# A two-layer recurrent network on one core per sequence: layer 0's FFN computed by features, and layer 1's normalisation with it

## The chip, the cores and the metric

The kernel runs on 8 cores of one Trainium2 chip. Each core takes one of the eight sequences (4096 tokens of 1024 features) through both layers, and the cores do not talk to each other. The metric is the device time of the slowest core in microseconds (us). The engines are named as the profile names them: PE is TensorE, PEld its weight loads, DVE is VectorE, ACT is ScalarE, POOL is GpSimd, SP is SyncE.

## The reference, cut to what matters

```python
# x: (8, 4096, 1024) float32; every kernel input is float32, layer 1's FFN weights int32
xn = _layernorm(x)                          # no scale, no bias
# layer 0: gates from block-diagonal linears, then a closed-form scan over time
gate_x = sigmoid(block_diag_linear(xn, w_in, b_in)); gate_a = sigmoid(block_diag_linear(xn, w_a, b_a))
a = minimum(exp(-gate_a * (softplus(a_param) + 0.001)), 1 - 1e-5)
s = closed_form_rnn_scan(xn * gate_x * sqrt(maximum(1 - a*a, 1e-5)), a)
g = silu(gelu(xn @ ternary(W1).T + b1) @ ternary(W2).T + b2)      # 1024 -> 4096 -> 1024
x = x + s * g
# layer 1
xn = _layernorm(x)
u  = _layer_norm(xn, gamma, beta)           # a second normalisation, over the first
zxbcdt = u @ W_in + b_in                    # z 2048 | x 2048 | B 64 | C 64 | dt 8 columns
s = xn + mamba2(...)                        # scan with 8 heads, silu(z), @ W_out + b_out
g = silu((silu(xn @ wg) * (xn @ wu)) @ wd)  # 1024 -> 3072 -> 1024, weights / 127
x = x + s * g
```

`ternary(W)` rounds to -1, 0 or 1 with a threshold from the mean of |W| over the whole matrix, so no matmul with W1 can begin before all of W1 has been read.

## The kernel before, in words

Everything is written out by hand in one function. There is no scheduler: each engine has a queue, and an instruction stands in it where the Python code appended it. Tokens (a semaphore and a count) say what an instruction waits for; `P.dma(queue, slot, out, in, *tokens)` puts a transfer on SP's or POOL's queue, and whatever stands behind it on that queue waits with it. Matrices are bf16 in SBUF; in 32 slots of 4 KB per partition lie first W1 as float32 (`raw`), then ternary W1 in the lower halves (`Lh`) and ternary W2 in the upper ones (`Hh`). The 4096 tokens go in 8 blocks of 512, a block in 4 tiles of 128.

**Start.** SP loads 4 tiles of x and the 32 tiles of W1; DVE and ACT sum absolute values (`w1_sum`, L281, L285). Between the sums block 0 is normalised, transposed by TensorE (L350) and its gates are computed (`a_gates`): for each of the 8 feature groups two gate matmuls, tanh into one of two buffers `thx`, and a store to `gt` in HBM by POOL. Block 0's gates stand between the sums, one after each third weight tile. A short chain on one partition splits b2 into three bf16 rows (L460 to L466). Then the threshold (L294), and W1 becomes ternary.

**Stage A**, per block: the up projection, L386: 32 feature tiles of 8 matmuls of 128 x 512, gelu by ACT into `hst`, stored to `h1` in HBM. The next block's normalisation and gates, and W2's sum and thresholding, run beside it. In the last block `b_early` runs block 0's recurrence and issues the first load of `h1`.

**Stage B**, the down projection by tokens: `b_down(n, hf)` for 32 tiles of 128 tokens and 2 halves of the features. The tile's `h1` is the stationary operand, W2 moves: 32 matmuls of 512 columns (L693) and one with three rows that adds b2 (L696). `b_tail` brings the recurrence's result, which lies by features, into token order with four fp32 transposes (L708), then silu on ACT (L715), product and residual on DVE (L716, L718), and stores x1 by tokens. Beside it DVE and ACT run the recurrence of the next block, one feature group per group of matmuls: `b_recA` (limited sum and difference, L555, L557), `b_recM` (L566 to L568) and `b_recC` (L576 to L580), with its gate inputs loaded by SP. POOL loads `Win` into the lower halves.

**Stage C**, 8 blocks: `c_ln` reads a tile of x1, takes its statistics (L760, L761), and derives both normalisations, 1/sqrt by pow on POOL (L768); `c_trans` transposes both results in bf16 by TensorE (L782), into `uT` for this stage and, by HBM, `xn1` for layer 1's FFN. For block 0 that happens in the last groups of stage B, for block b+1 in block b. A block's matmuls: dt and B/C columns (`c_small`, L882, L891), 16 groups for z (`c_z`, L915, evacuated by ACT to `zs`), 16 for x (`c_xs`, L932, evacuated by DVE to `xs`, L939), 8 matmuls of 512 columns each. In blocks 0 and 1 POOL also loads half of the gate and up weights (`gu_load`), cast from int32.

**Stages D and E**: the scan by chunks of 128 tokens with the matmuls of layer 1's FFN between them, then the two last projections and the sum. The change touches only the layout in which they read `xn1`.

The functions that the change touches:

## Time and profile before

| | |
|---|---|
| median of 3 runs | 2956.08 us (2955.19, 2956.08, 3278.76) |
| the profiled execution | 2955.45 us, its span on the slowest core 2953.6 us |
| spans of the eight cores | 2945.9 to 2953.6 us |
| granted TensorE clock, mean of a core | 0.987 to 0.995 of full |
| busy: PE, DVE, ACT, POOL | 2824.4, 1614.8, 1210.4, 334.3 us |
| moved by DMA | 515.04 MB, 174 GB/s over the span |
| start, to the threshold matmul | 0 to 87.96 us |
| stage A | to 606 us |
| stage B | 606.58 to 1110.70 us |
| stage C | 1110.70 to about 1630 us |
| gate loads and h1 loads, median to landing, whole run | 6.7 us, 6.4 us |
| casting weight loads issued from 1110 to 1200 us | 26 |
| waits on stores of xs before L939, whole run | 56.3 us in 35 |

The profile is one execution on the slowest core. An instruction's row names its line, engine, operation, and output<-inputs by the program's names. TensorE's matmuls are pipelined: a matmul of 512 columns is shown 0.38 us long, while eight of them start within 1.72 us, so what one costs is read from the starts. The brackets at a row's end tell how long the engine had been idle before it and what it waited for.

### The profile page before, as it was taken

How to read it: one execution, taken by the hardware profiler on the slowest of the kernel's cores; microseconds unless marked ns; L12 is line 12 of the kernel's file. 1: busy time of each engine (PE TensorE's matmuls, PEld its weight loads, DVE VectorE, ACT ScalarE, POOL GpSimd, SP SyncE). 2: the span in 40 equal slices, each digit the busy share in tenths (PEclk: the TensorE clock that was granted, in tenths of full speed). 3: DMA queues.
4: the chain of work that ended last, by engine and by line, in shares of the span. 5: the costliest groups of instructions: out<-in, count | busy, mean ns of one | idle time of the engine just before them, and what ended most of it. 6: DMA issues, size and time to landing. Idle time of an engine off the chain costs nothing.

```text
span 2953.6 us, 39109 instructions; the slowest of 8 cores (2945.9 to 2953.6 us)
## 1 busy us (share of the span) xinstructions
PE 2824.4 (96%) x14022; PEld 1330.5 (45%) x14222; DVE 1614.8 (55%) x2865; ACT 1210.4 (41%) x1806; POOL 334.3 (11%) x550
## 2 busy tenths in 40 slices
PE   2699999999999998999999999999999999999998
PEld 0244444444444444444444444444444444444443
DVE  4755576567777743444443666666666623333333
ACT  3665555777777733344432334333333300000000
POOL 1011121001110012100000122111111110000000
PEclk9999999999999999999999999999999999999999
DMA  9388887567897557533433666445564453433342
GB/s 285 112 251 269 270 266 240 165 210 222 229 242 227 191 185 166 147 108 119 127 113 111 194 172 182 154 141 171 164 182 139 150 161 136 144 137 128 143 146 76
DMA packets 269684, 515.04 MB, mean 174 GB/s; under 512 B 23476, under 2 KB 143028, under 8 KB 265272
## 3 DMA queue, kind: packets, MB, share of 16 engines
q1 hardware_dynamic: 208216, 338.16, 36.4%
q0 software_dynamic: 61280, 174.38, 20.5%
q8 instruction: 117, 1.92, 0.3%
q14 instruction: 71, 0.58, 0.1%
HBM read 359.89 MB, written 184.82 MB: 184 GB/s over the span
## 4 chain that ended last, share of the span: by engine, by line
PE 89%; DMA 4%; DVE 3%; ACT 2%; issue 1%; POOL 0%; SPq 0%; DVEq 0%; POOLq 0%; ACTq 0%
PE ps L693 14%; PE ps L386 14%; PE ps L1200 11%; PE ps L1206 11%; PE ps L1328 10%; PE ps L1341 7%; PE ps L932 7%; PE ps L915 6%; PE ps L708 1%; DMA zs<-zst 1%; PE ps L1082 1%; DMA gt<-thx 1%; PE ps L1088 1%; PE ps L782 1%; PE ps L350 1%
## 5 line engine op out<-in xcount | busy, mean ns | idle before, releaser
L386 PE MATMUL ps<-xnT,Lh 128*128 128x512 bf16 x2001 | 454.9, 382 | 9.6 <-ACT hst L390 3.8
L693 PE MATMUL ps<-Hh,h1s 128*128 128x512 bf16 x2000 | 449.3, 379 | 3.3 <-DMA h1s<-h 0.8
L1328 PE MATMUL ps<-Hh,hl 128*128 128x512 bf16 x1510 | 339.9, 379 | 1.4
L386 PEld LDWEIGHTS ps<-xnT,Lh 128*128 128x128 bf16 x2048 | 201.1, 98 | 241.7 <-issue 16.9
L693 PEld LDWEIGHTS ps<-Hh,h1s 128*128 128x128 bf16 x2048 | 200.1, 98 | 228.7 <-issue 1.5
L1203 ACT ACTIVATE sg<-ps 128x512 bf16<-128x512 f32 x192 | 111.3, 596 | 418.1 <-PE ps L1200 381.8
L1208 DVE TENSOR_TENSOR hgs<-sg,ps 128x512 bf16<-128x512 bf16 x192 | 131.5, 685 | 269.8 <-PE ps L1206 155.0
L1352 ACT ACTIVATE gx<-ps 128x512 f32<-128x512 f32 x64 | 38.2, 597 | 512.4 <-DVE sx L1354 501.6
L390 ACT ACTIVATE hst<-ps,cons 128x512 bf16<-128x512 f32 x256 | 172.7, 688 | 184.1 <-PE ps L386 161.6
L915 PE MATMUL ps<-uT,Lh 128*128 128x512 bf16 x1000 | 226.6, 381 | 7.9 <-ACT zst L918 5.4
L1328 PEld LDWEIGHTS ps<-Hh,hl 128*128 128x128 bf16 x1536 | 150.3, 98 | 181.2
L932 PE MATMUL ps<-Lh,uT 128*128 128x512 bf16 x1000 | 224.6, 380 | 4.7 <-DVE xst L939 3.1
L1351 DVE TENSOR_TENSOR sx<-sx,ps 128x512 f32<-128x512 f32 x64 | 44.1, 689 | 338.2 <-PE ps L1341 337.9
L1341 PE MATMUL ps<-Lh,yl 128*128 128x512 bf16 x756 | 185.5, 379 | 2.2 <-DMA Lh<-Wo 1.6
L1200 PE MATMUL ps<-xg,Hh 128*128 128x512 bf16 x768 | 181.8, 379 | 0.0
L1200 PE MATMUL ps<-xg,Lh 128*128 128x512 bf16 x768 | 181.7, 379 | 0.0
L1206 PE MATMUL ps<-xg,Hh 128*128 128x512 bf16 x768 | 181.4, 379 | 0.0
L1206 PE MATMUL ps<-xg,Lh 128*128 128x512 bf16 x768 | 181.4, 379 | 0.0
L939 DVE TENSOR_TENSOR xst<-ps,bx 128x512 bf16<-128x512 f32 x128 | 86.8, 690 | 133.9 <-PE ps L932 75.4
L915 PEld LDWEIGHTS ps<-uT,Lh 128*128 128x128 bf16 x1024 | 99.0, 98 | 124.4 <-issue 10.0
L932 PEld LDWEIGHTS ps<-Lh,uT 128*128 128x128 bf16 x1024 | 99.6, 98 | 122.4 <-issue 7.0
L101 POOL DMA_DIRECT2D hg<-hgs x96 | 73.0, 760 | 709.9 <-DVE hgs L1208 654.3
(209 smaller groups left out, 3683.7 us busy)
## 6 DMA issues: line engine op xcount, KB each, us to landing
gt<-thx POOLq DMA_DIRECT2D x64, 512.0 KB, 4.3
h<-hst SPq DMA_DIRECT2D x128, 256.0 KB, 3.9
wst<-W2T POOLq DMA_DIRECT2D x64, 512.0 KB, 5.7
h1s<-h SPq DMA_DIRECT2D x32, 1024.0 KB, 6.4
hg<-hgs POOLq DMA_DIRECT2D x96, 256.0 KB, 4.8
hl<-hg SPq DMA_DIRECT2D x32, 768.0 KB, 5.1
xt<-x SPq DMA_DIRECT2D x32, 512.0 KB, 7.0
raw<-W1T SPq DMA_DIRECT2D x32, 512.0 KB, 22.2
```

What stands on the lines that cost most here:

```text
L386: t = PE.do(lambda e, dc=dc: e.matmul(psum[i][:], Lh[(ft // 8) * 8 + dc][:, (ft % 8) * 128:(ft % 8 + 1) * 128], xnT[b % 2][:, dc, :], star ...
L390: pf[i] = ACT.do(lambda s: s.activation(hst[j][:, :, ft % 2, :], psum[i].rearrange("p (c t) -> p c t", t=128), AF.Gelu, bias=b1s[:, ft:ft ...
L693: PE.do(lambda e, f=f: e.matmul(psum[bk][:], H[:, f, :], Hh[f][:, hf * 512:(hf + 1) * 512], start=(f == 0), stop=False), h1_tok[n], pf[bk] ...
L915: t = PE.do(lambda e, dc=dc: e.matmul(psum[i][:], winp(dc, ft * 128, 128), U[:, dc, :], start=(dc == 0), stop=(dc == 7)), pf[i], tok=(dc = ...
L932: t = PE.do(lambda e, dc=dc: e.matmul(psum[i][:], U[:, dc, tt * 128:(tt + 1) * 128], winp(dc, 2048 + fb * 512, 512), start=(dc == 0), stop ...
L939: pf[i] = DVE.do(lambda v: v.tensor_add(xst[j][:], psum[i][:], bx[:, fb * 512:(fb + 1) * 512]), t, *xst_free[j], t_bx)
L1200: t = PE.do(lambda e, dc=dc: e.matmul(psum[i][:], gu(p, 0, dc, ft), X[:, :, dc, :], start=(dc == 0), stop=(dc == 7)), xg_tok[n], t_gu[p], ...
L1203: pf[i] = ts = ACT.do(lambda s: s.activation(sg[i][:], psum[i][:], AF.Silu, scale=1.0 / 127.0), t, sg_free[i], *endC)
L1206: t = PE.do(lambda e, dc=dc: e.matmul(psum[2 + i][:], gu(p, 1, dc, ft), X[:, :, dc, :], start=(dc == 0), stop=(dc == 7)), pf[2 + i], tok=( ...
L1208: pf[2 + i] = sg_free[i] = DVE.do(lambda v: v.tensor_mul(hgs[j][:, :, ft % 2, :], sg[i].rearrange("p (c t) -> p c t", t=128), psum[2 + i]. ...
L1328: td = PE.do(lambda e, f=f: e.matmul(psum[bd][:], hl[i][:, f, :], wd[f][:, sl], start=(f == 0), stop=(f == 23)), e_tok[(1, n)], t_wd, pf[b ...
L1341: to = PE.do(lambda e, f=f: e.matmul(psum[bo_][:], yl[i][:, f, :], wo[f][:, sl], start=(f == 0), stop=(f == 15)), e_tok[(0, n)], t_wo, pf[ ...
```

## The change

The down projection is turned round: W2's 128 x 128 tile is stationary and h1 moves, 256 tokens at a time, so that its result, like the recurrence's, lies by features. Two such groups of 32 matmuls share a PSUM bank. b2 becomes a bias of the silu, which now works inside PSUM; no bias matmul, no fp32 transposes of the recurrence. The residual x is read from a copy that the host has transposed (`xT`), and x1 is stored by features (`x1t`), in pieces of 1 KB. `h1` is kept in chunks of 256 tokens, stored in pieces of 1 KB rather than 512 bytes; two chunks of 2 MB lie in SBUF where W1 was.

The recurrence works in pairs of feature groups, with four gate buffers and four `rd` buffers from block 1 on and two `cl`; POOL copies the carries. The minimum in `b_recM` is gone.

Layer 1's normalisation works by features: `c_stat` reads a feature tile of x1, transposes it to tokens by TensorE in fp32, takes statistics of each 128 features, copies it out with ACT and stores it by tokens for the last stage; `c_rows` joins the statistics, transposes mean and both factors into rows, and brings them through HBM to all partitions; `c_app` reads the feature tile again and applies them on DVE. All of its loads and stores are on POOL's queue. In stage C the x groups come before the z groups, since the last z columns of `Win` are loaded only after stage B has freed h1's space. At the start there are four gate buffers for block 0, two of them in the space of x tiles 4 and 5, and the work on b2 is gone.

```diff
-    thx = [at(f"thx{i}", [128, 2, 512], F32, T0 + 4096 * i) for i in range(2)]
+    thx = [at(f"thx{i}", [128, 2, 512], F32, o)
+           for i, o in enumerate((T0, T0 + 4096, X0 + 16384, X0 + 20480))]
...
-        j = k % 2
+        j = k % 2 if b else k % 4
...
-    xfree[4] = xfree[5] = thx_free[0] = t_b2d
...
+    xfree[4], xfree[5] = thx_free[2:]
...
-            h1_tok[n] = P.dma(SP, s_h1[n % 2], h1s[n % 2][:], h1_d[n], h1_free[n % 2], *h1st[n // 4])
+            h1_tok[n] = P.dma(SP, s_h1[n % 2], h1s[n % 2], h1_d[n].rearrange("p (a f) t -> p a (f t)", a=8),
+                              h1_free[n % 2], *h1st[n // 2])
...
-    def b_down(n, hf):
-        g = n * 2 + hf
-        bk = g % 4
-        H = h1s[n % 2]
-        for f in range(32):
-            PE.do(lambda e, f=f: e.matmul(psum[bk][:], H[:, f, :], Hh[f][:, hf * 512:(hf + 1) * 512],
-                                          start=(f == 0), stop=False),
-                  h1_tok[n], pf[bk], t_w2[f], tok=False)
-        t = PE.do(lambda e: e.matmul(psum[bk][:], on3[:], b2s[:, hf * 512:(hf + 1) * 512], start=False, stop=True),
-                  t_on3, t_b2)
+    def b_down(g):
+
+        hb, p = divmod(g, 4)
+        bk = g % 6
+        H = h1s[hb % 2].rearrange("p a (f t) -> p a f t", t=256)
+        for e in range(2):
+            fb = 2 * p + e
+            for f in range(32):
+                t = PE.do(lambda q, f=f, fb=fb, e=e: q.matmul(
+                    psum[bk][:, e * 256:(e + 1) * 256], Hh[f][:, fb * 128:(fb + 1) * 128], H[:, f // 4, f % 4, :],
+                    start=(f == 0), stop=(f == 31)),
+                    h1_tok[hb], pf[bk], t_w2[f], tok=(f == 31 and e == 1))
...
+    def c_stat(b, k):
...
+        for c in range(4):
+            t = PE.do(lambda e, c=c: e.transpose(psum[bk][:, c * 128:(c + 1) * 128],
+                                                 xq[i][:, c * 128:(c + 1) * 128], idf[:]),
+                      xq_tok[j], pf[bk], tok=(c == 3))
+        for c in range(4):
+            td = DVE.do(lambda v, c=c: v.bn_stats(sst[:, c, k, :], psum[bk][:, c * 128:(c + 1) * 128]), t, st_prev[0])
+        sst_tok[b] = td
+        t = pf[bk] = ACT.do(lambda s: s.activation(xq[i][:], psum[bk][:], AF.Copy), td)
...
+    def c_app(b, k):
...
+        t = DVE.do(lambda v: v.tensor_sub(X[:], X[:], rows[:, 0, :]), xq_tok[j], row_tok[b])
+        tx = DVE.do(lambda v: v.tensor_mul(xb[k % 2][:], X[:], rows[:, 1, :]), t, *xb_free[k % 2])
+        tu = DVE.do(lambda v: v.tensor_mul(U, X[:], rows[:, 2, :]), *uT_free[b % 2])
...
+            if last == 3:
+                for k in range(4 * e, 4 * e + 4):
+                    c_app(0, k)
+                    if e == 0:
+                        c_load()
...
+    while win_todo:
+        b_winload(PE.last())
...
+    for _ in range(5):
+        c_load()
...
         for q in range(32):
...
+            if b + 1 < NB:
+                if q in (0, 1, 2, 3, 4, 9, 10, 11):
+                    c_stat(b + 1, (0, 1, 2, 3, 4, 9, 10, 11).index(q))
+                if q in (5, 6, 7, 8, 9, 13, 14, 15):
+                    c_load()
+                if q == 12:
+                    c_rows(b + 1)
+                if q in (20, 21, 23, 24, 26, 27, 29, 30):
+                    c_app(b + 1, (20, 21, 23, 24, 26, 27, 29, 30).index(q))
+                    c_load()
```

How the orders change, at three places. On TensorE in stage B, between two groups, before (`sv` holds the recurrence, `Hh` is W2):

```order
L693 MATMUL ps<-Hh_137,h1s_195 128x512
L693 MATMUL ps<-Hh_138,h1s_195 128x512
L696 MATMUL ps<-b2s,on_202 128x512
L708 MATMUL ps<-idf,sv_188 128x128 [waits s_act]
L708 MATMUL ps<-idf,sv_188 128x128 x3
L693 MATMUL ps<-Hh_107,h1s_195 128x512
L693 MATMUL ps<-Hh_108,h1s_195 128x512
```

and in the changed kernel, where `WW` holds h1:

```order
L708 MATMUL ps<-WW,Hh_139 128x256
L708 MATMUL ps<-WW,Hh_140 128x256
L708 MATMUL ps<-WW,Hh_109 128x256 [waits s_act]
L708 MATMUL ps<-WW,Hh_110 128x256
L708 MATMUL ps<-WW,Hh_111 128x256
```

Nothing stands between two groups any more, and each group is 32 matmuls of 256 columns. On POOL where stage B ends, before (from the last stores of x1 to the first weights of layer 1's FFN):

```order
L101 DMA x<-xr_198 128x512 [waits s_dve]
L101 DMA x<-xr_196 128x512 [waits s_dve]
L768 TENSOR_TENSOR ssm<-ssm,mhalf 128x2 [waits s_dve]
L101 DMA Hh_107<-wgT 128x1024 [waits s_pe]
L101 DMA Hh_108<-wgT 128x512
```

and changed (`xn<-xb` stores a normalised tile, `Lh<-Win` loads columns of z, `xq<-x1t` feature tiles of x1 for block 1's statistics):

```order
L101 DMA xn<-xb_219 128x512 [waits s_dve]
L101 DMA xn<-xb_220 128x512 [waits s_dve]
L101 DMA Lh_81<-Win 128x1024
L101 DMA Lh_82<-Win 128x1024
L101 DMA Lh_83<-Win 128x1024
L101 DMA Lh_84<-Win 128x1024
L101 DMA x1t<-xr_197 128x2x256 [waits s_dve]
L101 DMA x1t<-xr_195 128x2x256 [waits s_dve]
L101 DMA Lh_89<-Win 128x1024 [waits s_pe]
L101 DMA Lh_90<-Win 128x1024
L101 DMA Lh_91<-Win 128x1024
L101 DMA Lh_92<-Win 128x1024
L101 DMA xq_214<-x1t 128x512 [waits d_xo2,d_xo0]
```

Before, layer 1's loads had the queue to themselves from here on; now eight loads of `Win` and the tiles of x1 stand in it, behind stores that wait for DVE. On DVE in block 0 of stage C, changed, around `c_rows` (L814 to L829; L1032 evacuates an x group, L805 takes statistics):

```order
L805 BN_STATS sst<-ps 128x6 [waits s_pe]
L805 BN_STATS sst<-ps 128x6 x3
L1032 TENSOR_TENSOR xst_225<-ps,WWf 128x512 [waits s_pe,d_xs1]
L814 BN_AGGR smv<-sst 128x2 [waits s_dve]
L814 BN_AGGR smv<-sst 128x2 x3
L817 COPY st_237<-smv 128x4 [waits s_dve]
L818 COPY mu_all<-smv 128x4
L821 TENSOR_SCALAR ssm<-smv 128x4
L822 TENSOR_SCALAR ssm<-smv 128x4
L826 COPY r_all<-st_237 128x4 [waits s_pool]
L829 COPY srow<-ps 12x128 [waits s_pe]
L1032 TENSOR_TENSOR xst_224<-ps,WWf 128x512 [waits s_pe,d_xs0]
```

and on TensorE at the same place:

```order
L1027 MATMUL ps<-Lh_99,uT_221 128x512
L1027 MATMUL ps<-Lh_100,uT_221 128x512
L827 MATMUL ps<-idf,st_237 12x128 [waits s_pool,s_dve,s_act]
L1027 MATMUL ps<-wn_205,uT_221 128x512
L1027 MATMUL ps<-wn_206,uT_221 128x512
```

The statistics of a whole block are joined behind the evacuation of the group that TensorE has just finished, and TensorE's next group stands behind their transposition.

## Rows read from the trace of the kernel before

**Rows 1.** The page: busy time of each engine; chain that ended last, by engine

```profile
PE 2824.4 (96%) x14022; PEld 1330.5 (45%) x14222; DVE 1614.8 (55%) x2865; ACT 1210.4 (41%) x1806; POOL 334.3 (11%) x550
...
PE 89%; DMA 4%; DVE 3%; ACT 2%; issue 1%; POOL 0%; SPq 0%; DVEq 0%; POOLq 0%; ACTq 0%
```

**Rows 2.** Timeline of PE, down stage: start us, us, engine, line, operation, output<-inputs, count

```profile
809.80 7.07 PE L693 MATMUL ps<-Hh,h1s 128*128 128x512 bf16 x31
816.81 0.38 PE L696 MATMUL ps<-b2s,on 3*128 3x512 bf16 x1
817.12 0.66 PE L708 MATMUL ps<-idf,sv 128*128 128x128 f32 x4
817.61 7.07 PE L693 MATMUL ps<-Hh,h1s 128*128 128x512 bf16 x32
```

**Rows 3.** Timeline of all engines where the down stage begins

```profile
599.85 0.33 SPq L101 DMA_DIRECT2D h1s<-h  x1
...
606.58 7.07 PE L693 MATMUL ps<-Hh,h1s 128*128 128x512 bf16 x32 [0.78 <-DMA h1s<-h]
```

**Rows 4.** Timeline of PE where projection blocks begin

```profile
1110.70 1.67 PE L882 MATMUL ps<-uT,wtl 128*8 128x512 bf16 x7
...
1187.04 1.89 PE L882 MATMUL ps<-uT,wtl 128*8 128x512 bf16 x8
...
1565.97 1.89 PE L882 MATMUL ps<-uT,wtl 128*8 128x512 bf16 x8
```

**Rows 5.** DMA queues, window 1110 to 1200, and timeline of ACT there

```profile
q0 software_dynamic: 3616, 5.24, 37.4%
q1 hardware_dynamic: 8432, 8.69, 31.6%
...
1137.07 1.27 ACT L918 ACTIVATE zst<-ps,cons 128x512 bf16<-128x512 f32 x2 [6.87 <-DMA zs<-zst]
```

**Rows 6.** Timeline of the start; windows: engines' busy us (count), clock, DMA share, GB/s

```profile
69.72 1.27 ACT L367 ACTIVATE thx<-ps,cons 128x512 f32<-128x512 f32 x2 [8.49 <-DMA gt<-thx]
...
87.96 0.56 PE L294 MATMUL ps<-acc,onesf 128*128 128x1 f32 x2 [4.91 <-DVE acc L290]
...
78.00:82.00 4.00, 0.11 (x1) 0.10 (x1) 0.22 (x1) 0.94 (x2) 0.00 (x0) 1.00 0.98 395
```

**Rows 7.** Timeline of PE, 512, 256 and 128 columns; weight loads, ns min/median/max

```profile
1655.80 1.89 PE L1206 MATMUL ps<-xg,Hh 128*128 128x512 bf16 x8
1657.52 0.27 PE L1082 MATMUL ps<-Cx,stb 128*128 128x256 bf16 x1
1657.63 0.28 PE L1088 MATMUL ps<-sct,xsc 128*128 128x128 bf16 x2
...
1657.96 1.89 PE L1200 MATMUL ps<-xg,Hh 128*128 128x512 bf16 x8
...
L1082 PEld LDWEIGHTS ps<-Cx,stb x256: 95/98/98, 1630.0 to 2377.9; 128*128 128x128 bf16 x128
```

**Rows 8.** Timeline of DVE in the down stage; landing times of the gate loads

```profile
642.01 1.28 DVE L555 TENSOR_TENSOR_SCAN cl<-gv,car,par 128x512 f32<-128x512 f32 x1
643.33 0.69 DVE L557 TENSOR_TENSOR rd<-cl 128x512 f32<-128x512 f32 x1
...
644.01 0.69 DVE L576 TENSOR_TENSOR sv<-sv,gv 128x512 f32<-128x512 f32 x1
...
645.20 1.28 DVE L580 TENSOR_TENSOR_SCAN sv<-rd,sv,sv 128x512 f32<-128x512 f32 x1
...
DMA to landing us min/median/max: 4.4/6.9/9.8
```

**Rows 9.** Timeline where the down stage ends; one group of PE by line

```profile
1087.57 0.21 DVE L761 BATCH_NORM_AGGREGATE smv<-sst 128x2 f32<-128x12 f32 x1
...
1088.99 0.81 DVE L769 TENSOR_SCALAR ub<-xc,smv,ssm 128x1024 bf16<-128x1024 f32 x1 [0.90 <-POOL ssm L768]
...
L782 PE MATMUL ps<-idb,ub 128*128 128x128 bf16 x256 | 19.5, 219 | 0.0
```

506 lines of the change are left out of this document (280 added, 226 removed).

## The prediction, made before the changed kernel ran

> **What bounds the kernel now.** I read the page first: TensorE is busy 96% of the span, and 89% of the chain that ended last is matmuls [rows 1]. So only three things count: columns that TensorE streams, instructions that stretch them, and stretches in which it waits. I went through the stages with the timeline.
>
> The down stage is a stream: 32 matmuls of 512 columns take 7.01 us (809.80 to 816.81), then come a bias matmul and four fp32 transposes, and the next group starts 7.81 us after the last [rows 2]. 64 such groups and some layer norm fill 606.58 to 1110.70, 504.1 us [rows 3, 4]. The projection blocks behind it start at 1110.70, 1187.04 and, the eighth, 1565.97 [rows 4]: the first takes 76.3 us, the next six 378.9 us, 63.2 each. So the first loses 13 us. There ScalarE stood 6.87 us on a store of zs, while 26 casting weight loads held the q0 queue for 37.4% of 90 us [rows 5]: 1.3 us of all engines for each. At the very start TensorE does next to nothing until the threshold matmul at 87.96; ScalarE had waited 8.49 us for a gate buffer to be stored [rows 6].
>
> The durations are of the profiled execution (2955.45 us; the median of the runs is 2956.08, so the two are interchangeable).
>
> **1. The start.** Two gate buffers become four, and 4.5 us of VectorE work on b2 go. But behind the gates stand the loads of W1: the DMA engines are at 0.98 up to 82 [rows 6]. By 82 us they had moved the weights, six gate stores and two early x tiles. The x tiles queue behind the weights, the two gate stores now pulled ahead compete with them, so the last weight tile lands at 79 to 82. A sum, the total and the threshold follow in about 2 us: 82.5 for 88, **-5.5** (from -2 to -9). The x tiles 4 and 5 now wait for the gates' stores, near 85 us; they are used after 105, so this costs nothing.
>
> **2. Into the down stage.** The first h1 load was issued at 599.85, and TensorE started at 606.58 after a wait of 0.78 us [rows 3]. It is 2 MB now instead of 1: at the 3.3 us per MB of q1 (8.69 MB in 31.6% of 90 us) [rows 5], that is 3 us later. **+2.5** (0 to 5).
>
> **3. The down stage.** 2048 matmuls of 512 columns become 4096 of 256, each with its own weight load; 64 bias matmuls and 256 transposes go. The price of a 256-column matmul with full weights stands in the trace: two of them and four of 128 columns, 1024 columns in six instructions, take 0.44 us (1657.52 to 1657.96), against 1.72 us for eight of 512 [rows 7]. By columns that is 0.110 us for 256; half of a 512 is 0.1075. I take 0.1095, nearer to the first: 4096 x 0.1095 = 448.5 us. No row shows such a stream lasting more than six instructions, so the range keeps 0.1075 (440) to 0.115 (471).
> Added: 32 fp32 transposes for block 0's statistics at 0.49/4 us [rows 2]: 3.9. They come four tiles in a row on two PSUM banks, so the third waits for four statistics and a copy of the first, about 1.75 us, twice: 3.5 (0 to 6). The transposition in c_rows sits behind a group of 7 us and its inputs are ready: 0.
> Then the end. VectorE has the normalisation of eight tiles behind the tail of group 61: three fp32 operations each, 0.69 us [rows 8], so 8 x 2.07 = 16.6 us, from 2.4 us into the last pair of groups, and its bf16 stores stand on POOL's queue behind four weight loads, 2.5 us more. The pair takes 14 us, so the first projection waits 8.5 us with the copy (0 to 12). Sum: 448.5 + 3.9 + 3.5 + 8.5 = 464.4 against 504.1, **-39.7**.
> On VectorE a pair of steps costs 2 x 1.97 (scan, difference), 2 x 2.47 (product, addition, scan) and 2 x 1.4 (tail) = 11.6 us [rows 8], inside 14. Copies of carries go to POOL, which is 11% busy. Six PSUM banks give the tails two pairs of slack.
>
> **4. Projection block 0.** POOL's order is the point: the last eight Win tiles stand there behind the stores of the normalised tiles and the last tails, and the five x1 tiles that block 1's statistics need stand behind those. Eight tiles at 1.67 us (1.3 scaled from the mean of 202 KB to 256) are 13 us from about 7 us behind the stage's end; the x1 tiles land at about 24. TensorE has 12 us of its own before (8.5 waiting, 3.5 of c_small), so it waits **12 us** at the first transposition. After that each of the 16 x steps asks for a weight load (1.3), an x1 store or load (0.9) and an xs store (0.4): 2.6 to 2.7 us of DMA against 1.73 of TensorE, 43 us; the z steps ask for 2.0, 32 us; c_rows 3. Block: 3.5 + 12 + 43 + 3 + 32 = 93.5 against 76.3, **+17.2** (from -10, if all of it is hidden, to +54).
>
> **5. Blocks 1 to 6.** Transposes: 64 of bf16 (0.076 us busy each, 19.5 us for 256) against 32 of fp32 at 0.12 [rows 2, 9]: nothing. But c_rows puts one transposition between two groups of TensorE that needs a chain begun after the group before it: its evacuation on VectorE (0.8 with the wait), four aggregates, two copies, two small operations, and pow on POOL. The same chain for one tile took 1.42 us, 1087.57 to 1088.99 [rows 9]; three more aggregates are 0.6. So 2.8 us in each, x 6 = **+16.8** (0 to 25). The other work fits: VectorE has 1.5 us in a step of 2.2 that carries statistics.
>
> Moved without effect: in front of D and later, layouts alone change. Sum: -5.5 + 2.5 - 39.7 + 17.2 + 16.8 = -8.7, so 2955.45 - 8.7 = **2946.7 us**. What the FFN gives, the new layer norm takes back.
>
> **Rivals.**
> *A, all hidden.* Start -9, down stage 448.5 + 3.9 (-51.7), block 0 at 66 us (-10), rows free: -71, **2884 us**. For it: TensorE is the only full engine. Against it: the orders above.
> *B, VectorE's loop through the gate loads bounds the down stage; the side of slower.* A gate buffer is freed by the product of pair m and refilled for the scan of pair m+2, the first thing VectorE does next. The loop is 8.1 us of VectorE's work and the load: from a load of 5.9 us on it exceeds 14. The loads took 4.4, 6.9 and 9.8 us (minimum, median, maximum) there [rows 8], beside 1 MB loads ahead of them on the same queue. At 6.9 a pair takes 15.0: 30 x 1.0 = +30, **2977 us**; at 9.8, +117, 3064. Against it: the h1 loads go out before every second pair only, and with nothing ahead the minimum applies.
> *C, DMA binds the projections.* Stores of xs have two buffers of one step each. If each of the eight pairs of x steps is held 6.87 us longer, as ScalarE once was by a store [rows 5], they take 28 + 55 = 83 us, 40 more than in the sum, and block 1 half of that: 2947 + 60 = **3007 us**. For it: half the buffer of zs, in the time of the densest loads. Against it: POOL issues the weight loads behind its x1 work, so they thin out when the steps slow down.
> *D, weight loads don't hide.* A weight load of such a matmul lasts 98 ns [rows 7]. Shown bare, it adds 4096 x 0.098 = 401 us: **3348 us**. The row of six instructions in 0.44 us speaks against it: six loads alone would be 0.59. The Trainium skill says, in "TensorE: Matmul & The Clock Gate", under The mechanism, that a weight load overlaps matmuls in flight only when its row group differs; all here use all rows, and by that rule this change would be a disaster. The trace disagrees already in its 512-column stream. The same page gives, under Back-to-back issue gap, sustained pairs of about 81 ns for 128 columns and 131 ns for 512; an estimate from that page for 256 is 98 ns between them, which would make the sum 47 us less. The trace disagrees with that too: its 512 columns take 0.215 us.
> That the diff does not do what it says: the orders show the matmuls, so 2%, with no time.
>
> **Chances.** Main case 48%, A 17%, B 18%, C 13%, D 2%, other 2%. The main case's own range is 2925 to 2970. The range for 8 in 10 leaves out the ends of A and B and C's worse half: **2890 to 2990**. 2% of the time is 59 us, what a measurement here separates surely: faster than 2897 takes nearly all of A, 15%; slower than 3015 takes B's long loads, part of C, and D: 8%; within, 77%.
>
> **What would show it.** Step 1: the threshold matmul at 82 to 83. Step 3: 64 matmuls of the new down line in 7.0 us, no idle time between groups; if VectorE's scans there wait for gv for over 2.4 us a pair, B is on. A wait of 8 us before the first projection, on VectorE or ScalarE (uT). Step 4: 12 us of TensorE at the first transposition of xq, waiting for its load, and idle TensorE on xst in block 0. Step 5: some 3 us of idle TensorE in front of the transposition of the statistics, seven times, and projection blocks of 66 us. The prediction is wrong if the blocks stay at 63, or if 256 columns take more than 0.115 us.

## The result, and the profile of the changed kernel

The changed kernel takes 3022.77 and 3013.82 us, beside 2955.19 to 2957.74 before: a ratio of 1.021, with a 95% interval of 1.0172 to 1.0247. It is slower, by some 62 us; whether by more than 2% the runs leave open. (Some executions of either kernel, in which the cores of a die show a lower clock, take up to 3346.66 us; the times below are all of the others.) The prediction was 2947, with a range of 2890 to 2990. The profiled execution is the one of 3022.77 us, span 3020.9, so it stands 67.3 us above the profiled one of before.

First the page: totals, the granted clock in 40 slices, the chain that ended last by engine, and two groups of instructions.

```profile
PE 2802.6 (93%) x15474; PEld 1509.7 (50%) x15702; DVE 1632.2 (54%) x2875; ACT 1136.7 (38%) x1686; POOL 571.3 (19%) x987
...
PEclk7799999999999988999999999999999999999999
...
PE 70%; DMA 14%; DVE 9%; ACT 2%; SPq 2%; issue 2%; POOL 1%; DVEq 0%; POOLq 0%; ACTq 0%
...
L708 PE MATMUL ps<-WW,Hh 128*128 128x256 bf16 x4096 | 451.8, 274 | 5.3 <-DMA WW<-h 5.3
...
L556 DVE TENSOR_TENSOR_SCAN cl<-gv,cl,par 128x512 f32<-128x512 f32 x64 | 81.9, 1279 | 100.9 <-DMA gv<-gt 99.2
```

TensorE is busy 22 us less than before [rows 1] in a span 67 us longer, and matmuls hold 70% of the chain that ended last, for 89% before. The clock row has two 8s where block 0 of the projections lies, and two 7s at the start; the same row of before has 9s in all 40 places. Then the boundaries, from TensorE's timeline (start us, us, line, tiles, count, idle before and its releaser):

```profile
607.63 4.56 PE L708 MATMUL ps<-WW,Hh 128*128 128x256 bf16 x21 [4.76 <-DMA WW<-h]
...
889.61 56.05 PE L708 MATMUL ps<-WW,Hh 128*128 128x256 bf16 x512 [0.24 <-DMA WW<-h]
...
1023.83 2.18 PE L801 MATMUL ps<-idf,xq 128*128 128x128 f32 x8 [7.85 <-DMA xq<-x1t]
...
1056.69 0.27 PE L827 MATMUL ps<-idf,st 128*12 128x128 f32 x1 [1.83 <-DVE r_all L826]
...
1092.31 3.57 PE L976 MATMUL ps<-uT,wtl 128*8 128x512 bf16 x8 [14.39 <-ACT ps L721]
...
1109.50 1.09 PE L801 MATMUL ps<-idf,xq 128*128 128x128 f32 x4 [11.38 <-DMA xq<-x1t]
...
1199.98 3.57 PE L976 MATMUL ps<-Lh,wtl 128*8 128x512 bf16 x8 [3.21 <-ACT Lh L846]
...
1633.60 1.89 PE L976 MATMUL ps<-Lh,wtl 128*8 128x512 bf16 x8
```

They answer to [rows 3, 4]. The ledger for the slowest core, core 6 in both, with the prediction's terms:

| part | predicted | measured | from |
|---|---|---|---|
| start, to the threshold matmul | -5.5 | -3.7 | 87.96 to 84.26 |
| from there to the down stage | +2.5 | +4.7 | the stage starts at 607.63 for 606.58 |
| down stage, to block 0 | -39.7 | -19.4 | 484.7 us for 504.1 |
| projection block 0 | +17.2 | +31.3 | 107.7 for 76.3 |
| blocks 1 to 6 | +16.8 | +54.7 | 433.6 for 378.9 |
| the rest | 0 | -0.3 | 1387.3 for 1387.6 |
| sum | -8.7 | +67.3 | |

Cores differ more than they did. In the kernel before, all reach their eighth block between 1555.9 and 1566.0; in the changed one between 1603 and 1634. Already where the down stage ends the changed kernel's cores lie from 1070.4 to 1092.6, for 1106.4 to 1111.1 before; the slowest core's stage is 19.4 us shorter, the median one's 27.1 (476.6 for 503.7). So the median core is used beside the slowest from here on; for it block 0 takes 104.7 us (before 72.6), block 1 76.8 (63.3), and blocks 2 to 6 70.7 each (63.0).

### The profile page after: what moved, and what is told of

Read it like the earlier page. It is cut to its first block, busy times and chain, and to the rows that moved or that the text cites. A ratio compares the mean times of both kernels' runs of the same rounds, so it can differ in the third digit from the quotient of the medians.

```text
span 3020.9 us, 42623 instructions; the slowest of 8 cores (2994.9 to 3020.9 us)
## 1 busy us (share of the span) xinstructions
PE 2802.6 (93%) x15474; PEld 1509.7 (50%) x15702; DVE 1632.2 (54%) x2875; ACT 1136.7 (38%) x1686; POOL 571.3 (19%) x987
## 4 chain that ended last, share of the span: by engine, by line
PE 70%; DMA 14%; DVE 9%; ACT 2%; SPq 2%; issue 2%; POOL 1%; DVEq 0%; POOLq 0%; ACTq 0%
PE ps L387 13%; PE ps L1297 11%; PE ps L1303 11%; PE ps L1426 11%; PE ps L1439 7%; PE ps L1008 6%; PE ps L1027 5%; DMA gv<-gt 5%; DMA xs<-xst 3%; SPq L101 2%; DVE cl L556 1%; DMA xr<-xT 1%; DVE xr L733 1%; PE ps L1175 1%; DMA xq<-x1t 1%
## 5 line engine op out<-in xcount | busy, mean ns | idle before, releaser
L708 PE MATMUL ps<-WW,Hh 128*128 128x256 bf16 x4096 | 451.8, 274 | 5.3 <-DMA WW<-h 5.3
L708 PEld LDWEIGHTS ps<-WW,Hh 128*128 128x128 bf16 x4096 | 402.3, 98 | 54.6 <-issue 6.2
L1032 DVE TENSOR_TENSOR xst<-ps,WWf 128x512 bf16<-128x512 f32 x128 | 87.7, 690 | 185.1 <-DMA xs<-xst 94.6
L1012 ACT ACTIVATE zst<-ps,cons 128x512 bf16<-128x512 f32 x128 | 87.0, 685 | 185.7 <-PE ps L1008 148.3
L556 DVE TENSOR_TENSOR_SCAN cl<-gv,cl,par 128x512 f32<-128x512 f32 x64 | 81.9, 1279 | 100.9 <-DMA gv<-gt 99.2
L1303 PEld LDWEIGHTS ps<-xg,Hh 128*128 128x128 bf16 x768 | 75.2, 98 | 90.6
L1439 PEld LDWEIGHTS ps<-Lh,yl 128*128 128x128 bf16 x768 | 75.1, 98 | 90.6
```

Of the source, the lines that this page charges most:

```text
L556: tc = DVE.do(lambda v: v.tensor_tensor_scan(L[:, 2:514], G[:], lim, L[:, 1:2], op0=ALU.add, op1=ALU.min), gv_tok[n], ci_tok[n])
L708: t = PE.do(lambda q, f=f, fb=fb, e=e: q.matmul(psum[bk][:, e * 256:(e + 1) * 256], Hh[f][:, fb * 128:(fb + 1) * 128], H[:, f // 4, f % 4, :],
L1303: t = PE.do(lambda e, dc=dc: e.matmul(psum[2 + i][:], gu(p, 1, dc, ft), X[:, dc, :], start=(dc == 0), stop=(dc == 7)), pf[2 + i], tok=(dc ...
L1439: to = PE.do(lambda e, f=f: e.matmul(psum[bo_][:], yl[i][:, f, :], wo[f][:, sl], start=(f == 0), stop=(f == 15)), e_tok[(0, n)], t_wo, pf[ ...
```

## Where the time went

**The steady blocks.** This is TensorE in block 3 where the statistics are done, then VectorE and POOL in the same microseconds:

```profile
1376.63 1.89 PE L1027 MATMUL ps<-Lh,Lh 128*128 128x512 bf16 x8
1382.88 0.27 PE L827 MATMUL ps<-idf,st 128*12 128x128 f32 x1 [4.36 <-DVE r_all L826]
1382.99 5.30 PE L1027 MATMUL ps<-wn,Lh 128*128 128x512 bf16 x15
```

```profile
1378.63 0.69 DVE L1032 TENSOR_TENSOR xst<-ps,WWf 128x512 bf16<-128x512 f32 x1 [0.67 <-PE ps L1027]
1379.24 1.05 DVE L814 BATCH_NORM_AGGREGATE smv<-sst 128x2 f32<-128x48 f32 x4
...
1382.55 0.17 DVE L826 COPY r_all<-st 128x4 f32<-128x4 f32 x1 [1.85 <-POOL st L824]
...
1380.86 1.66 POOL L824 TENSOR_TENSOR st<-ssm,mhalf 128x8 f32<-128x8 f32 x1 [0.95 <-DVE ssm L822]
```

and pow on POOL in the kernel before:

```profile
1088.25 0.71 POOL L768 TENSOR_TENSOR ssm<-ssm,mhalf 128x2 f32<-128x2 f32 x1 [1.39 <-DVE ssm L766]
```

The last group of matmuls before the transposition ends near 1378.5. Its evacuation, four aggregates (1.05), small operations and pow (1.66 for eight columns; it was 0.71 for two) take until 1382.9: 4.36 us idle for the 2.8 of the prediction. Behind it, 15 matmuls take 5.30 us where 16 usually take 3.62: the clock has gone to its lower level, 0.426 us a matmul for 0.216 (1.2 for 2.4 GHz), and comes back within them. By the starts (the next group begins at 1388.12) that is 1.7 us more.

By the mean of the eight cores a block of 2 to 6 is 7.7 us longer than before. Of these 4.4 are the wait at this transposition and 0.7 are other waits (before, TensorE had none in these blocks). The other 2.5 are a longer time in which it works: the mean granted clock of these blocks is 0.964, for 1.00.

**Block 0.** Its DMA queues answer to [rows 5]; then two waits from the same stretch, 1092 to 1200 (total, times, longest):

```profile
q0 software_dynamic: 7689, 16.91, 74.2%
q1 hardware_dynamic: 5311, 3.59, 10.8%
```

```profile
DVE xst L1032 <- DMA xs<-xst: 27.5, 7, 6.7
...
ACT zst L1012 <- DMA zs<-zst: 17.2, 5, 8.7
```

q0 took 37.4% of 16 engines for 90 us, and takes 74.2% of 108 us now. TensorE waited 11.38 us for the first x1 tile (12 were predicted). VectorE and ScalarE also stood on their stores of xs and zs, and TensorE in turn on them.

## The experiments

All are edits of the changed kernel, 3018 us. Its ratio of 1.021 has an interval of +-0.004, so a difference of under some 11 us is not told apart by times; the lengths of the blocks (median of 8 cores, one profile each) are the finer gauge. Seven kernels, the changed one among them, have the same program up to the end of the down stage, and their median cores still reach block 0 anywhere from 1080 to 1092: for that point one profile says little. Steps are those of the 32 in a projection block (16 for x, 16 for z), q in the code.

### The transposition one group later

```diff
                 if q == 12:
-                    c_rows(b + 1)
+                    c_rows(b + 1)          # up to pow
+                if q == 13:
+                    c_rows2(b + 1)         # from the copy to r_all on
```

> Changed kernel: about 3018 us. Here the statistics' small chain (aggregates, pow) still starts at step 12 of each block, but the transposition of its result and all behind it come one group of matmuls later, in blocks 1 to 7's preparation. Theory (the wait costs itself and the clock behind it): TensorE's idle 4.4 us in front of that transposition goes, and with it the matmuls of twice the length behind it (some 2 us); blocks 2 to 6 fall from about 70 to 64 us, in all -38 to -45, so 2973 to 2980. Rival 1 (the long matmuls there have another cause, such as the loads in flight): only 7 x 4.4 = -31, so 2987. Rival 2 (the wait comes back further down, since the row tiles land later for the normalisation): under -10, so 3008 or more.

3012.12 us, ratio 1.0177 (1.0159 to 1.0194). Block 3 on its slowest core:

```profile
1384.99 0.37 PE L836 MATMUL ps<-idf,st 128*12 128x128 f32 x1 [2.63 <-DVE r_all L835]
1385.15 3.48 PE L1036 MATMUL ps<-wn,Lh 128*128 128x512 bf16 x8
```

The wait fell by the one group, 1.73 us, to 2.63, and here the lower clock stayed: eight matmuls in 3.48. Blocks 2 to 6: 68.0. The gain in time is the second rival's, under 10 us, but its reason, a wait that comes back further down, is not the main one here: the chain is as long as read above, and one group does not cover it.

Over the eight cores and blocks 2 to 6 there are 40 such waits in each kernel. In the changed kernel the clock fell to its lower level behind all 40, of 4.35 to 5.62 us. Here it fell behind 27 of 40, of 2.63 to 2.93 us; it fell behind some of exactly 2.63 and not behind others.

### Work in the wait

```diff
+        if b:
+            for f in range(16):
+                PE.do(matmul(psum[5], winp(0, 2048, 128), winp(1, 2048, 512)))   # read by nobody
         t = PE.do(lambda e: e.transpose(psum[7][0:12 ...
```

> Computes the same; in front of each transposition of the statistics in the projection blocks TensorE has 16 extra matmuls of 512 columns (3.5 us) whose result nobody reads, so that it works in most of the 4.4 us in which it was idle. Theory (the matmuls of 0.42 us behind the wait are long because TensorE had been idle): they return to 0.216 us, each block gets some 2 us shorter, about -14 in all, so 3004. Rival (they are long for another reason, or the idle time has nothing to do with it): no gain, 3018; if the wait is not 4.4 us of pure idling but shorter in other blocks, the extra matmuls cost up to 5 us.

3018.56 us, 1.0200 (1.018 to 1.022). Blocks 2 to 6 fell from 70.7 to 68.7, block 1 from 76.8 to 75.7. TensorE in block 3 of this kernel; then the same 16 us of the changed kernel and of this one in the view by windows, which ends with the granted clock, the DMA share and GB/s:

```profile
1378.80 3.62 PE L829 MATMUL ps<-wn,wn 128*128 128x512 bf16 x16
1383.33 0.27 PE L831 MATMUL ps<-idf,st 128*12 128x128 f32 x1 [0.91 <-DVE r_all L826]
1383.44 3.62 PE L1031 MATMUL ps<-wn,Lh 128*128 128x512 bf16 x16
```

```profile
1376.00:1392.00 16.00, 11.59 (x48) 5.12 (x48) 5.83 (x21) 1.19 (x2) 7.27 (x10) 0.89 0.58 164
```

```profile
1376.00:1392.00 16.00, 14.62 (x69) 6.79 (x70) 7.18 (x24) 1.66 (x3) 7.28 (x10) 1.00 0.54 161
```

The only thing added is work, the wait is down to 0.91, and the 16 matmuls behind it take 3.62 us: the lower clock came from the idle time, and it cost 2 us a block. That the blocks became shorter by adding 16 matmuls shows it; the whole time does not (its block 0 began 10 us later, within the spread named above). On all eight cores the clock stayed up behind the 38 waits of 0.9 to 1.1 us, and its mean in blocks 2 to 6 is 0.999. Without waits and without the extra matmuls (3.45 us) these blocks take 63.5 us at that clock, for 63.0 before: TensorE's own work is some 0.6 us longer, which the prediction had put at nothing.

### Three groups later, two steps earlier, one step earlier

The same split with the second part at step 15:

> As the kernel in which the transposition of the statistics came one group of matmuls later, but three groups later (5.2 us of matmuls). One group took the idle time from 4.4 to 2.6 us, exactly by the 1.73 us of the group, and the half clock stayed. Theory (a chain of 4.4 us from the last group's end, and the half clock goes only with the whole wait): no idle time in front of the transposition, no matmuls of 0.42 us in blocks 2 to 6, each about 6.2 us shorter than the changed kernel's 70.5 (median core): 64; in all -40, so 2980. Rival (the row tiles then land too late and the normalisation delays the next block's first projection): waits of 2 to 4 us on uT at block starts, so 2995 to 3005.

Runs of 3013.52, 3014.38 and 3031.42 us, 1.0214 (1.0146 to 1.0283); blocks 2 to 6: 67.9. The mechanism of the rival came out, with a longer time than it had named. TensorE, then VectorE in that block:

```profile
1385.08 0.27 PE L836 MATMUL ps<-idf,st 128*12 128x128 f32 x1
...
1416.89 3.54 PE L985 MATMUL ps<-uT,wtl 128*8 128x512 bf16 x8 [2.18 <-ACT uT L855]
```

```profile
1387.09 0.27 DVE L838 COPY srow<-ps 12x128 f32<-12x128 f32 x1
...
1397.01 0.69 DVE L849 TENSOR_TENSOR xq<-xq,rows 128x512 f32<-128x512 f32 x1 [5.78 <-DMA rows<-st]
...
1415.21 0.69 DVE L851 TENSOR_TENSOR uT<-xq,rows 128x512 bf16<-128x512 f32 x1
```

No wait before the transposition, but 2.18 before the next block's first projection, at the lower clock again (3.54 for 8). From the row copy (1387.09) it is 10 us until the rows have been stored and read back to all partitions (1397.01), then 19 us of normalisation. Both lie on the path to that projection. By the mean of the eight cores 2.4 us of wait a block stand there.

So the whole chain was put forward, the second part three groups behind the first:

```diff
-                if q in (0, 1, 2, 3, 4, 9, 10, 11):    # c_stat
-                if q in (5, 6, 7, 8, 9, 13, 14, 15):   # c_load
-                if q == 12:                            # c_rows
-                if q in (20, 21, 23, 24, 26, 27, 29, 30):   # c_app
+                if q in (0, 1, 2, 3, 4, 7, 8, 9):
+                if q in (4, 5, 6, 7, 8, 11, 12, 13):
+                if q == 10:                            # c_rows2 at 13
+                if q in (18, 19, 21, 22, 24, 25, 27, 28):
```

> In blocks 1 to 7's preparation the last three tiles of statistics come at steps 7, 8, 9 instead of 9, 10, 11, the small chain at 10 for 12, the transposition of its result at 13 (three groups after the chain begins), the normalisation from step 18 for 20; x1's loads two steps or one earlier with them. The last run showed the wait of 4.4 us reappear as one of 2 to 3.5 us, with half clock behind it, on uT at the start of the next block. Theory (there is one chain per block: statistics, rows 10 us, eight tiles of normalisation 19 us, next block's first projection; only an earlier start shortens it): neither wait, blocks 2 to 6 at 64 us for 70.5 and 68: -6.5 x 6 and some of block 0, so 2975 to 2980. Rival (VectorE's and POOL's queues or x1's loads can't keep up with the earlier steps): waits on xq at steps 7 to 9 of 2 us or more, blocks of 67 or more, 2995 or more.

Runs of 3002.97, 3008.16 and 3016.62 us, 1.0181 (1.0151 to 1.021). Blocks 2 to 6: 68.6. The rival again, now at the other end (waits of TensorE from 1275 to 1610 us: total, times, longest; and its timeline):

```profile
PE ps L801 <- DMA xq<-x1t: 16.3, 5, 4.1
```

```profile
1298.38 0.63 PE L801 MATMUL ps<-idf,xq 128*128 128x128 f32 x4 [2.81 <-DMA xq<-x1t]
1298.85 1.89 PE L1036 MATMUL ps<-Lh,uT 128*128 128x512 bf16 x8
...
1364.61 0.94 PE L801 MATMUL ps<-idf,xq 128*128 128x128 f32 x4 [3.15 <-DMA xq<-x1t]
1365.34 3.30 PE L1036 MATMUL ps<-Lh,Lh 128*128 128x512 bf16 x8
```

Between the two, with statistics at steps 8 to 10, x1 loads at 3, 4, 5, 7, 8, 12, 13, 14, the chain at 11 and 14, normalisation from 19:

> As the kernel with statistics two steps earlier, but one: the last three tiles at steps 8, 9, 10, the chain at 11, the transposition of its result at 14, the normalisation from 19; the x1 loads for the three tiles at steps 3, 4, 5 for 4, 5, 6 there. There the wait had moved to the x1 load of the sixth tile, 3 us in each block (14 us in four to five of them), and blocks were 68. Theory (one chain per block with no slack on either side; now both ends have 1.7 us more): no wait of TensorE over 1 us in blocks 2 to 6, full clock, 64 to 65 each; 2990. Rival (the load of the sixth tile waits for the store of the first, which frees its buffer, so issuing it earlier gains nothing, and the chain behind gets the wait): blocks of 67 to 68 again, 3000.

Runs of 3001.59 and 3002.57 us, beside 2954.83 to 2955.93 of before. Blocks 2 to 6: 67.1, between theory and rival. TensorE's waits from 1275 to 1610:

```profile
PE ps L801 <- ACT xq L807: 5.8, 4, 2.4
PE ps L985 <- ACT uT L855: 4.2, 3, 2.0
PE ps L1017 <- ACT zst L1021: 4.1, 5, 1.4
...
PE ps L836 <- POOL st L824: 0.6, 1, 0.6
```

The wait at the transposition is 0.6 us in all. What is left is spread over several places, none above 2.4 us. Of the 7.7 us a block that the change costs, this order gives back 3.6; some 4 remain. By the mean of the cores 3.0 of them are waits: 1.1 of a transposition of xq for its PSUM bank, which ScalarE's copy frees, 1.0 of the next block's first projection for its normalised tiles, 0.5 for ScalarE behind its stores of zs, and 0.4 others. The rest is TensorE's longer work and a little of the clock. So only a part of what remains lies at the two ends of the chain.

### Order and density of the loads

The last 12 weight loads behind the x1 loads of block 1 (and the fifth x1 buffer free at the last scan):

```diff
-        if last >= 2:
-            for _ in range(4):
-                b_winload(dn_tok[2 * (NC - 2) - 1])
...
-    while win_todo:
-        b_winload(PE.last())
...
-    xq_free[4] = endB
+    xq_free[4] = (rec_tok[NB * 8 - 1],)
     uT_free[1] = endB
     for _ in range(5):
         c_load()
+    while win_todo:
+        b_winload(PE.last())
```

> The last 12 casting weight loads for the projections are issued on POOL behind the stores of the normalised tiles and the five x1 loads of block 1, and the fifth x1 buffer is freed by the last scan, not by the end of the stage. Theory (order on POOL's queue costs the first projection block): TensorE's 11.4 us at the first transposition of xq go, the 14.4 us before the first projection fall to 9 or so; block 0 from 107.7 to about 93: -15 to -20, so 2998 to 3003. Rival (the DMA engines are full there whatever the order): the weights land later and the z steps wait in their place; under -5, so 3013 or more.

3031.83 us, 1.0241 (1.0223 to 1.0259): worse than its rival. Slowest core:

```profile
1096.55 3.57 PE L973 MATMUL ps<-uT,wtl 128*8 128x512 bf16 x8 [10.20 <-ACT ps L721]
...
1107.69 1.09 PE L801 MATMUL ps<-idf,xq 128*128 128x128 f32 x4 [4.62 <-DMA xq<-x1t]
...
1146.89 1.08 PE L801 MATMUL ps<-idf,xq 128*128 128x128 f32 x4 [17.43 <-DMA xq<-x1t]
```

The first wait for x1 fell from 11.38 to 4.62 and the one before block 0 to 10.20, as thought. Then TensorE stood 17.43 us for the next x1 load: it was issued at 1137.72, when a store of x1 by tokens had freed its buffer, and that store stood behind the twelve weight loads (POOL waited 7.00 us for it). A wait was moved, and grew.

The GLU weights' loads, thinner:

```diff
-            if b < 2 and q % 2 == 0 or b == 0 and q < 16:   # gu_load
+            if 0 < b < 6 and q % 4 == 0:
```

> The 32 casting loads of the GLU weights that are issued in the first two projection blocks are issued at every fourth step of blocks 1 to 4 instead. Theory (density of DMA work in block 0 makes the waits on stores of xs, zs and xn): block 0 falls from 107.7 by 10 to 15 us and block 1 from 79.1 by some 5: -15 to -20, so about 3000. Rival (these waits are the latency of a store with two buffers, not density): no change of block 0, 3018.

Runs of 3015.43, 3019.55 and 3025.71 us; 1.0203 (1.0181 to 1.0226). Block 0 fell from 104.7 to 85.1, more than expected, but blocks 2 to 6 rose from 70.7 to 73.6. 24 loads less in block 0 (twelve of 256 KB and twelve of 128 KB) are 19.6 us, 0.8 us for each, and where they went, blocks 2 to 4, they cost 0.6 each (blocks 2 to 6 are 2.9 longer each). TensorE still waited 12.7 us for the first x1 tile: density and order are two terms of block 0.

Both together, the 12 weight loads one by one in steps 0 to 11 of block 0, the GLU loads at steps 16 to 19 of every block:

> The last 12 weight loads for the projections go one by one in front of the first 12 steps of block 0, behind the five x1 loads, and the GLU weights' 32 loads go to steps 16 to 19 of every block, where POOL's queue has no x1 load due. Theory (a casting weight load costs TensorE some 0.75 us wherever an x1 load for the statistics stands behind it, and nothing elsewhere): both waits of block 0 at the first transpositions go, block 0 falls from 104 to about 85 or less, the others stay at 70.5: -20 to -25, so 2996. Rival (total DMA work is what counts): block 0 falls as much as blocks 1 to 7 gain, as when the GLU loads were spread: 3018 to 3025.

Runs of 3007.94 to 3012.87 us, 1.0171 (1.0151 to 1.0191). Block 0: 90.7, block 1: 71.1, the others 72.2, 1.5 more than before the edit: a time between the theory and the rival. Steps 16 to 19 were not free either. That the rows' load and the normalisation's x1 loads stand near them is a likely reason, not a shown one.

The x1 loads on SP's queue:

> The loads of x1 (fp32, no cast) go on SP's queue and the hardware's rings instead of POOL's. Theory (the x1 tiles are late because they stand behind casting weight loads and stores on POOL's queue): the waits on xq in block 0 (14 us) and at the start of the statistics in the down stage (8 us) go, block 0 falls by 15 us: 3003. Rival 1 (they are late because the DMA engines are full): no change. Rival 2 (SP stops for a free x1 buffer, and the stores of xs and zs behind it hold VectorE and ScalarE): blocks of over 75 us, slower than 3030.

```diff
-        xq_tok[j] = P.dma(POOL, s_xq[i], ...)
+        xq_tok[j] = P.dma(SP, s_xq[i], ...)
```

One run, 3030.48, so its time says little. On the slowest core the wait for x1 at the first transposition of block 0 is gone, as the theory says (one of 1.08 us comes at the fifth), but in the down stage the first x1 tile is waited for 13.85 us, for 7.85, the first projection for 17.79, for 14.39, and ScalarE stopped the small transpositions of block 0 for 5.33. Block 0: 99.2, the others 70.5. The queue's order makes the wait of block 0; taking x1 out of it moves the loss.

### The end of the down stage

```diff
-        if i % 2 == 0 and i > 1:
-            b_load(i // 2 + 1)
...
             for n in (m + 2, m + 3):
                 b_svload(n)
+        if i % 2 == 0 and i > 1:
+            b_load(i // 2 + 1)
```

> In the down stage the 2 MB load of h1 is issued behind the gate loads of its step instead of ahead of them. Theory (VectorE's loop through the gate loads is longer than a pair of groups, 14.07 us, since every second pair's gate loads stand behind h1; TensorE doesn't stop in the stream because of its six banks, but VectorE is late at the end): VectorE's wait on gate loads falls from 99 us to under 60, the first x1 load for the statistics goes out earlier, the 8 us on it and part of the 14 us in front of the first projection go: -10 to -15, so 3005. Rival (VectorE's lateness costs nothing, x1's own loads are late by the DMA engines): -0 to -3, 3016.

Runs of 3070.07, 3070.36 and 3074.24 us, 1.0379 (1.0355 to 1.0402). The waits of the stream (640 to 1060; engine, tile, line, total, times, longest), of the changed kernel first, then of this one:

```profile
DVE cl L556 <- DMA gv<-gt: 62.6, 29, 5.0
...
DVE xr L733 <- DMA xr<-xT: 7.0, 6, 5.0
```

```profile
DVE xr L733 <- DMA xr<-xT: 93.5, 14, 8.6
...
PE ps L708 <- DMA WW<-h: 43.3, 12, 7.8
DVE cl L556 <- DMA gv<-gt: 25.5, 26, 1.7
```

VectorE's wait for gate loads fell to less than half, as the theory said, and the time rose all the same. SP takes its queue in order; a load of h1 that stands behind gate loads is issued when VectorE has freed a gate buffer (in this stretch SP waited 300.5 us for VectorE, for 234.4). So TensorE now waited for h1, 43.3 us in 12. The edit also put the 2 MB in front of the loads of the residual, and VectorE waited 93.5 us for those, for 7.0. Its waits for loads grew in all, so the shorter wait at the gates is no proof of a shorter loop. What the run shows is that TensorE can be stopped by SP's queue as soon as h1 stands behind loads that wait for VectorE; how much of the changed kernel's late end comes from the gate loads it does not show.

The normalisation of block 0 earlier in VectorE's order (four tiles behind the groups of the last pair but one, four inside the last):

> At the end of the down stage the normalisation of block 0's first four tiles is put one group pair earlier in the program, the last four go half a pair earlier; everything else as changed. Theory (the 14 us in front of the first projection come from the order on VectorE's queue: eight tiles of normalisation stand behind the tails of the last groups, and their stores behind four weight loads): the wait falls to 5 us or less, and -10 in the time, 3010. Rival (the rows arrive too late for it, or the wait moves to the x1 loads of block 1, which then stand in the same place behind weight loads): block 0's start moves by under 3 us, or block 0 gets longer by as much, 3018 to 3022.

3032.56 us, 1.0280 (1.0226 to 1.0333), slower. The wait before block 0 is 20.4 us on its slowest core, and one of 8.7 came up at the transposition of block 1's statistics. VectorE before block 0:

```profile
1073.61 0.69 DVE L840 TENSOR_TENSOR xq<-xq,rows 128x512 f32<-128x512 f32 x1 [12.81 <-DMA xq<-x1t]
...
1097.31 0.69 DVE L841 TENSOR_TENSOR xb<-xq,rows 128x512 bf16<-128x512 f32 x1 [6.69 <-DMA xn<-xb]
```

It stood 12.8 us at the first tile, which with the rows had not landed, the tails of two groups behind it; then 6.69 for a store of xn. So an earlier place on VectorE's queue does not shorten the 14.4 us. Taking the four weight loads from in front of the stores does: the wait was 10.2 above and is 8.2 in the kernel with the three edits below. VectorE's third normalised tile, in the changed kernel and in that one:

```profile
1078.30 0.69 DVE L841 TENSOR_TENSOR xb<-xq,rows 128x512 bf16<-128x512 f32 x1 [5.15 <-DMA xn<-xb]
```

```profile
1072.49 0.69 DVE L850 TENSOR_TENSOR xb<-xq,rows 128x512 bf16<-128x512 f32 x1 [0.50 <-DMA xn<-xb]
```

Its stops on stores of xn there are 6.9 us in all, and 1.0.

### Together

With the edits of the two "earlier" kernels (two steps; normalisation in the down stage), the 12 spread loads, and the GLU loads four at a time at step 31:

> Both edits of this call, with the 12 last projection weight loads spread over block 0's first 12 steps (they took 15 to 20 us from blocks 0 and 1 before) and the 32 GLU loads at the last step of each block, four at a time, so that the next x1 load on POOL's queue comes seven us later. If the causes are separate, the gains add: start of block 0 10 us earlier, block 0 at 85, block 1 at 66, blocks 2 to 6 at 64: 3018 - 10 - 19 - 11 - 40 = 2938, which beats the kernel before (2956). Rival (the DMA engines' total load binds once the waits are gone): blocks of 67 to 68, 2965.

Runs of 2995.93 and 2997.38 us, 1.0138 (1.0114 to 1.0162); only its time is used. That is the time of neither side: the theory had 2938, the rival 2965. Without the normalisation's move, which alone had cost, and with statistics one step earlier:

> The edit of the other kernel of this call, the 12 projection weight loads spread over the first 12 steps of block 0, and the GLU loads four at a time at the last step of each block. Theory (additive: block 0 and 1 had lost 11 to 16 us by order, the chain 6 a block): block 0 at 90, block 1 at 68, others 65: 2975 to 2980. Rival (the GLU loads at the block's end delay the x1 loads of the next block's statistics): the others stay at 68 and the time at 2990 to 2996.

2987.31 us, 1.0108 (1.0088 to 1.0129): 31 us faster than the changed kernel, and still slower than before. Block 0: 87.0, block 1: 70.2, the others 68.8. TensorE's longest waits at the end of the down stage and in block 0 of its slowest core (total, times, longest):

```profile
PE ps L979 <- ACT ps L721: 8.2, 1, 8.2
PE ps L801 <- DMA xq<-x1t: 6.8, 3, 4.1
```

The gains of block 0 (18) and 1 (7) add to a part of the steady ones (2 a block; 3.6 without the GLU loads between them). Last, rows and xn by SP's queue on top:

> The kernel with the three edits (2987 us), and the stores of the rows and of xn and the broadcast load of the rows on SP's queue instead of POOL's. What is left there: waits of 2 to 3 us on uT at the start of a block and at the third of the late tiles, blocks of 68.5. Theory (the chain's part from the rows to uT is lengthened by POOL's queue: 3 us until the rows' store has landed, stalls of VectorE on xn's stores, two buffers): the rows land 1 to 2 us earlier and the stalls on xn go, blocks of 66: -12, 2975. Rival (SP then waits for the rows and the xn tiles, the stores of xs and zs behind it are late, and ScalarE and VectorE stall in their place): no gain or a loss, 2985 to 3010.

Runs of 2991.87, 2996.02 and 2999.29 us, 1.0133 (1.0109 to 1.0158); blocks 2 to 6: 69.4. The rival: VectorE's wait for the stores of xs there is 69.1 us in 31 waits (1275 to 1590), for 49.7 in 31 without this edit. No version here beats the kernel before.

## Why the prediction was wrong, step by step

Between the forecast, -8.7, and the measured +67.3 lie 76 us: 38 in step 5, 20 in step 3, 14 in step 4 and 4 in the first two.

**Step 5, the failed one.** "2.8 in each" of blocks 1 to 6 was +16.8; it is +54.7. The mechanism, a transposition that waits for a chain through pow, was right and its place too. Its size was not: 4.36 us, 26.2 in six blocks, since pow of eight columns takes 1.66 us and was priced by the one of two. The larger part of what is missing is a term that the sum did not have. Outside all waits TensorE works 19.1 us longer in these six blocks. Its own longer work is some 3 of them, an estimate from the 0.6 a block of the kernel with extra matmuls; the other 16 are the lower clock behind the waits. And "the other work fits" was false: 9.4 us are other waits, 4.7 of them in block 1 for x1 tiles and for the bank that a statistics tile frees, and with the wait at the transposition moved away, others came at both ends. Statistics, rows (10 us) and normalisation (19 us) fill a block with little slack, which the counts of VectorE's work alone did not show.

**Step 4, block 0.** +31.3 for +17.2. The 12 us at the first transposition came (11.38), for the reason given. The 16 x steps with c_rows took 50.4 us for 46, and 4.46 of them are the wait for pow. The z steps were mis-sized most, 40.1 us for 32: TensorE waited 10.2 us there, 5.2 behind ScalarE's stores of zs and 3.2 for the last normalised tile. The first small matmuls took 5.8 for 3.5, at the lower clock. In the whole block TensorE works 7.0 us longer than before outside its waits, and the granted clock was 0.84 from 1110 to 1150 and 0.91 to 1200, for 0.97 and 0.95 before; the sum had no term for it. The edit of the GLU loads shows 0.8 us for each casting load in this block. Rival C had the stores as its mechanism, with 40 us more in block 0 and 20 in block 1; measured on top of the sum are 14 and 12.

**Step 3, the down stage.** The stream is as priced: 512 matmuls of 256 columns in 56.05 us, 0.1095 each, and 5.3 us idle in all of L708. What was wrong stands around it. The x1 tiles for the first statistics were taken to be there; they were issued at 1014, VectorE being late, and TensorE waited 7.85 us, with 3.9 in four smaller waits (3.5 predicted for all). One of the four, 1.83, is the transposition in c_rows, whose inputs were said to be ready. Before the first projection it is 14.39 for 8.5: VectorE stood 6.9 us on stores of normalised tiles, the first of them behind four weight loads (the sum had 2.5), and in the kernel with three edits, where these loads are gone, the wait is 8.22, about the 8.5 of the sum. The waits together are 26.1 for 12.0, 14 of the 20 us missing; the remaining 6 are matmuls at the lower clock behind these waits, as the 21 of 607.63 in 4.56 us (0.217 each). On the median core the stage is 12.6 us over the sum, not 20: the wait for the first x1 tile goes from nothing to 8.7 us over the cores, while the one before the first projection is 12.8 to 15.3 on all.

**Rival B** was half right. VectorE did wait for gate loads, 62.6 us in 29 waits over the stream, 2.2 us each, just under the 2.4 that the prediction had named as the sign, and TensorE never stopped for it inside the stream. Its cost, if it had one, stands at the end, where the x1 tiles need VectorE's last result; how much of the 7.85 us there is due to the gate loads no run shows.

**Steps 1 and 2.** The threshold came 3.7 us earlier, inside the range; ScalarE and VectorE wait for W1's tiles there, as said, and the last comes at 82.6. The stage before ended at 602.87 for 605.80 [rows 3], so 2.9 of it arrived. The 2 MB load then gave back 4.0: TensorE waited 4.76 us at 607.63 for 0.78. The sum had 2.5.

**Rival D** did not come: 4096 pairs, each with its own weight load of 98 ns, take 0.1095 us each, which leaves no room for a load that is not hidden. The rule in the Trainium skill's "TensorE: Matmul & The Clock Gate", The mechanism, that a load overlaps only where its row group differs, does not hold for this stream. The same section also lets a load run ahead when it goes to the background weight buffer, and the hidden loads here agree with that. The same page, under Back-to-back issue gap, also has a formula for isolated matmuls, columns by 2.4 GHz and 2.5 ns; an estimate from it for 256 columns is 109.2 ns, and here a stream with weight loads takes 109.5, so it fits better than the page's sustained pairs.

## What to carry to other kernels

When an operand is produced for the next block while the current one runs, write its whole chain down as a line of time, DMA round trips and small operations included, and compare it with the block: engines that are half busy say nothing of it. Price a small operation by its width and its engine, and price every wait of TensorE of some microseconds by what follows it too, here half as much again (2 us behind one of 4.4). And where one wait is removed, look at once at both ends of the same chain.

## What was not expected of the hardware

- A gap of a few microseconds brings the lower clock: after 2.63 us idle eight matmuls of 512 columns took 3.48 us, after 4.36 us 15 took 5.30. Behind waits of 4.35 us or more in the changed kernel it was so 40 times of 40, behind 2.63 to 2.93 us 27 of 40, behind 0.9 to 1.1 us never in 38. The same length does not decide it alone: after 2.81 us idle at 1298.38 the eight behind took 1.89, after 3.15 at 1364.61 they took 3.30.
- pow on POOL takes 1.66 us for 128x8 and 0.71 for 128x2.
- A casting load (256 or 128 KB) cost TensorE some 0.8 us in block 0, 19.6 us for 24, and 0.6 where the 24 went instead, in blocks 2 to 4.
- Seven executions of what is one program up to there differ by up to 12 us in when the median core ends the down stage, and the cores of one execution by up to 22 (1070.4 to 1092.6). In the kernel before they differ by 5 (1106.4 to 1111.1).
